# Orders of their own for the last batches of a scan, expert and feed-forward kernel

## The reference

```
delta = softplus(x @ Wd + bd);  B = x @ WB + bB;  C = x @ WC + bC      # 16 states s
h_s   = clip(exp(min(delta * A_s, 2)) * h_s + clip(delta * B_s, -2, 2) * x, -100, 100)
y     = sum_s h_s * C_s + x * D                                       # scan over 1024 tokens
e     = argmax softmax(y @ Wr + br)                                   # 4 experts, the best one
moe   = (silu(y @ up_e + b) @ down_e + b) * weight
x1    = layernorm(x + layernorm(y + moe) * ln_w + ln_b)
out   = layernorm(x1 + (silu(x1 @ wg) * (x1 @ wu)) @ wdn)             # hidden size 384
```

## Time and profile before

| | |
|---|---|
| runs | 948.23, 947.88, 947.88 us; median 947.88 |
| profiled execution | 944.45 us, its span 942.3 us |
| busy in the span | PE 69%, PEld 54%, DVE 73%, ACT 60%, POOL 65% |
| mean granted TensorE clock | 0.825 |
| memory | 157 GB/s over the span |

### The profile page before, as it was taken

The page is one execution under the profiler, slowest core; times in us unless marked ns, Lnnn a source line. Parts: engine busy times, 40 slices in busy tenths (PEclk is TensorE's granted clock), DMA queues, the critical chain, the costliest instruction groups (busy, mean ns, idle before and its releaser), DMA issues.

```text
span 942.3 us, 14125 instructions
## 1 busy us (share of the span) xinstructions
PE 646.6 (69%) x4244; PEld 512.7 (54%) x4296; DVE 687.4 (73%) x1330; ACT 563.5 (60%) x1052; POOL 608.4 (65%) x516
## 2 busy tenths in 40 slices
PE   3345657875889378956896598947894699168244
PEld 1234536763778257844785387725773488157233
DVE  3699998799779987898879977998789784221131
ACT  5553355694867578684859486757864485165223
POOL 0367557578956898488937895689838883650551
PEclk8587767995899779975999589967998599679766
DMA  3333355754556437653665465643755374325200
GB/s 99 120 139 123 133 171 172 262 178 151 191 200 208 157 117 254 191 196 97 209 205 174 154 198 195 203 157 115 254 174 185 107 238 155 107 85 176 62 3 22
DMA packets 82085, 149.30 MB, mean 158 GB/s; under 512 B 9404, under 2 KB 51144, under 8 KB 81992
## 3 DMA queue, kind: packets, MB, share of 16 engines
...
HBM read 132.80 MB, written 15.40 MB: 157 GB/s over the span
## 4 chain that ended last, share of the span: by engine, by line
POOL 26%; DVE 22%; PE 21%; issue 15%; ACT 10%; DMA 3%; another core or an unknown queue 1%; SPq 1%; POOLq 0%; ACTq 0%; DVEq 0%
DVE state L1136 10%; POOL prod L1163 7%; POOL rows_in L1184 4%; PE psU L647 3%; POOL rstd L1206 3%; DVE psB L1127 3%; PE psD L550 3%; ACT hid L798 3%; PE psT L661 3%; DVE moe L1078 2%; PE psU L686 2%; POOL attn L1228 2%; POOL moe L1222 2%; POOL moe L1220 2%; DVE bst L1095 2%
## 5 line engine op out<-in xcount | busy, mean ns | idle before, releaser
L1163 POOL TENSOR_TENSOR prod<-state,c_wide 128x1024 f32<-128x1024 f32 x128 | 308.1, 2416 | 85.1 <-DVE state L1136 66.1
L520 PE MATMUL psB<-parts,sel 128*128 128x512 bf16 x204 | 95.3, 469 | 139.0 <-DVE state L1136 136.9
L1127 DVE TENSOR_TENSOR psB<-dx,psB 128x512 f32<-128x512 f32 x256 | 166.8, 688 | 12.9 <-PE psB L520 2.6
L1136 DVE TENSOR_TENSOR_SCAN state<-decay,state,psB 128x512 f32<-128x512 f32 x128 | 163.9, 1280 | 14.3 <-issue 0.5
L526 PE MATMUL psY<-ident,prod 128*128 128x128 f32 x1024 | 155.5, 305 | 12.1 <-DVE state L1136 6.3
L1136 DVE TENSOR_TENSOR_SCAN state<-decay,psB 128x512 f32<-128x512 f32 x128 | 155.4, 1214 | 0.2
L759 ACT ACTIVATE decay<-delta,a_sb 128x1024 f32<-128x1024 f32 x128 | 141.0, 1143 | 16.9 <-DVE state L1136 11.6
L526 PEld LDWEIGHTS psY<-ident,prod 128*128 128x128 f32 x1024 | 138.3, 160 | 17.1 <-POOL prod L1163 8.8
L798 ACT ACTIVATE hid<-psU,weights 128x128 f32<-128x128 f32 x352 | 99.5, 370 | 49.3 <-PE psU L647 45.5
L520 PEld LDWEIGHTS psB<-parts,sel 128*128 128x128 bf16 x256 | 26.5, 106 | 186.7 <-DVE state L1136 180.5
L661 PE MATMUL psT<-weights,hid 128*128 128x128 f32 x704 | 97.5, 281 | 0.0
...
## 6 DMA issues: line engine op xcount, KB each, us to landing
c_wide<-c_rows SPq DMA_DIRECT2D x128, 512.0 KB
...
```

The source lines that it names most:

```text
L520: pe.matmul(tokens(psB, c, h), sel[:, s, :], parts[:, c.n % 2, h * HALF:h * HALF + c.hw], start=True, stop=True).then_inc(b_ready, 1)
L1127: v.tensor_tensor(tokens(psB, c, h), dx[:, n % 2, h * HALF:h * HALF + c.hw], tokens(psB, c, h), ALU.mult).then_inc(inp_ready, 1)
L1136: v.tensor_tensor_scan(state[:, g % NSTATE, t0:t0 + c.hw], decay[:, g % NDECAY, t0:t0 + c.hw], tokens(psB, c, h), before, ALU.mult, ALU.ad ...
L1163: g_.tensor_tensor(prod[:, g % NPROD, w], state[:, g % NSTATE, w], c_wide[:, g % NC, w], ALU.mult).then_inc(prod_ready, 1)
```

## The change

Each of the five lists at the end gets content: the tasks of the last batch's scans and all that follows. On TensorE, ScalarE, VectorE and GpSimd the resulting sequence first differs from the one before in the last batch (`6 up 0` where `7 add 6` was, `7 decay 11` where `5 x_high 0` was, `5 stats 1 1` where `7 scan 10` was, `5 gather 1` where `7 prod 1` was). SyncE's list at the end begins with `5 c 6`, and its first difference is `6 over` and `4 weights 10` where `5 c 15` and `4 weights 8` were, while batch 5 is scanned. The numbers count from the end: -1 is batch 7, -4 batch 4. Cut to what the prediction speaks of:

```
 PE_LAST = [
...
+    (-3, "ff_up", 1, 2), (-1, "spread", 14, 1), (-3, "ff_up", 1, 3), (-3, "ff_up", 1, 4), (-3, "ff_up", 1, 5),
+    (-3, "ff_down", 1), (-2, "up", 8), (-3, "ff_part", 1, 0), (-2, "down", 7), (-3, "ff_part", 1, 1),
+    (-3, "ff_part", 1, 2), (-1, "spread", 15, 0), (-2, "up", 9), (-2, "down", 8), (-1, "spread", 15, 1),
+    (-1, "add", 12), (-2, "up", 10), (-2, "down", 9), (-2, "down", 10), (-1, "add", 13), (-1, "add", 14),
...
+    (-1, "up", 8), (-2, "ff_part", 1, 1), (-1, "up", 9), (-1, "down", 8), (-1, "up", 10), (-1, "down", 9),
+    (-2, "ff_part", 1, 2), (-1, "down", 10), (-1, "x_turn", 0), (-1, "x_rest", 0), (-1, "ff_up", 0, 0),
...
 ]
 ACT_LAST = [
...
+    (-2, "result", 1), (-2, "sort_copy", 2), (-1, "decay", 13), (-1, "decay", 14), (-1, "decay", 15),
+    (-2, "result", 2), (-3, "norm", 1, 1), (-2, "silu", 3), (-2, "result", 3), (-2, "silu", 4), (-3, "norm", 0, 2),
...
+    (-1, "sort_copy", 0), (-1, "silu", 0), (-1, "result", 0), (-1, "sort_copy", 1), (-1, "silu", 1), (-1, "silu", 2),
+    (-1, "result", 1), (-1, "sort_copy", 2), (-1, "router_exp"), (-1, "result", 2), (-1, "silu", 3),
...
 ]
 DVE_LAST = [
...
+    (-3, "stats", 0, 2), (-1, "scan", 12), (-1, "scan", 13), (-3, "ff_mul", 1, 0), (-3, "ff_mul", 1, 1),
+    (-1, "scan", 14), (-3, "ff_mul", 1, 2), (-3, "stats", 1, 2), (-1, "scan", 15), (-1, "router_shift"),
+    (-1, "slots"), (-2, "combine", 0), (-2, "stats", 0, 0), (-2, "stats", 0, 1), (-2, "combine", 1),
...
 ]
 POOL_LAST = [
...
+    (-3, "rstd", 1, 0), (-1, "prod", 6), (-3, "affine", 1), (-1, "prod", 7), (-1, "prod", 8), (-1, "prod", 9),
...
+    (-3, "rstd", 1, 2), (-1, "prod", 14), (-1, "prod", 15), (-2, "gather", 0), (-2, "gather", 1), (-2, "gather", 2),
+    (-2, "gather", 3), (-2, "gather", 4), (-1, "scatter", 0), (-2, "gather", 5), (-2, "rstd", 0, 0),
+    (-2, "gather", 6), (-2, "gather", 7), (-2, "affine", 0), (-1, "scatter", 1), (-1, "scatter", 2),
...
 ]
 SP_LAST = [
+    (-3, "c", 6), (-3, "c", 7), (-3, "c", 8), (-4, "rows"), (-3, "c", 9), (-3, "c", 10), (-4, "weights", 3),
+    (-3, "c", 11), (-4, "weights", 4), (-4, "x"), (-3, "c", 12), (-4, "weights", 5), (-3, "c", 13),
+    (-4, "weights", 6), (-3, "c", 14), (-4, "weights", 7), (-2, "over"), (-4, "weights", 10), (-3, "c", 15),
+    (-4, "weights", 8), (-4, "weights", 9), (-2, "c", 0), (-4, "store", 0), (-4, "store", 1), (-1, "xT"),
+    (-4, "store", 2), (-2, "c", 1), (-2, "c", 2), (-2, "c", 3), (-2, "c", 4), (-2, "c", 5), (-3, "weights", 0),
+    (-3, "weights", 1), (-3, "weights", 2), (-2, "c", 6), (-2, "c", 7), (-3, "rows"), (-2, "c", 8), (-2, "c", 9),
...
 ]
```

More of the change, by code:

```diff
@@ L144 @@
 PE_LAST = [
+    (-2, "yT_turn"), (-1, "spread", 2, 0), (-1, "spread", 2, 1), (-1, "skip"), (-2, "logits"), (-1, "spread", 3, 0),
+    (-1, "add", 0), (-1, "spread", 3, 1), (-1, "add", 1), (-2, "rank"), (-1, "spread", 4, 0), (-1, "add", 2),
+    (-1, "spread", 4, 1), (-1, "spread", 5, 0), (-1, "spread", 5, 1), (-1, "add", 3), (-1, "spread", 6, 0),
+    (-1, "spread", 6, 1), (-1, "add", 4), (-1, "spread", 7, 0), (-1, "spread", 7, 1), (-1, "spread", 8, 0),
+    (-3, "x_turn", 0), (-1, "spread", 8, 1), (-3, "x_rest", 0), (-3, "ff_up", 0, 0), (-3, "ff_up", 0, 1),
@@ new lines @@
+    (-3, "ff_up", 0, 2), (-3, "ff_up", 0, 3), (-1, "spread", 9, 0), (-3, "ff_up", 0, 4), (-1, "add", 5),
+    (-1, "spread", 9, 1), (-3, "ff_up", 0, 5), (-2, "sort_turn", 0), (-2, "up", 0), (-1, "add", 6), (-2, "up", 1),
+    (-2, "sort_turn", 1), (-1, "spread", 10, 0), (-1, "spread", 10, 1), (-2, "down", 0), (-2, "up", 2),
+    (-2, "down", 1), (-2, "sort_turn", 2), (-1, "spread", 11, 0), (-1, "add", 7), (-1, "spread", 11, 1),
+    (-2, "down", 2), (-1, "add", 8), (-2, "up", 3), (-3, "ff_down", 0), (-1, "add", 9), (-3, "ff_part", 0, 0),
@@ new lines @@
+    (-1, "spread", 12, 0), (-3, "ff_part", 0, 1), (-3, "ff_part", 0, 2), (-2, "up", 4), (-2, "down", 3),
+    (-1, "spread", 12, 1), (-1, "add", 10), (-1, "add", 11), (-2, "down", 4), (-2, "up", 5), (-1, "spread", 13, 0),
+    (-1, "spread", 13, 1), (-3, "x_turn", 1), (-2, "up", 6), (-3, "x_rest", 1), (-2, "down", 5),
+    (-1, "spread", 14, 0), (-3, "ff_up", 1, 0), (-3, "ff_up", 1, 1), (-2, "down", 6), (-2, "up", 7),
+    (-3, "ff_up", 1, 2), (-1, "spread", 14, 1), (-3, "ff_up", 1, 3), (-3, "ff_up", 1, 4), (-3, "ff_up", 1, 5),
@@ new lines @@
+    (-2, "ff_up", 0, 5), (-1, "sort_turn", 0), (-1, "up", 0), (-1, "up", 1), (-1, "sort_turn", 1), (-1, "down", 0),
+    (-1, "up", 2), (-1, "down", 1), (-1, "sort_turn", 2), (-1, "down", 2), (-1, "up", 3), (-2, "ff_down", 0),
+    (-2, "ff_part", 0, 0), (-2, "ff_part", 0, 1), (-2, "ff_part", 0, 2), (-1, "up", 4), (-1, "down", 3),
+    (-1, "up", 5), (-1, "down", 4), (-2, "x_turn", 1), (-1, "up", 6), (-2, "x_rest", 1), (-1, "down", 5),
+    (-2, "ff_up", 1, 0), (-2, "ff_up", 1, 1), (-1, "down", 6), (-1, "up", 7), (-2, "ff_up", 1, 2), (-2, "ff_down", 1),
@@ new lines @@
+    (-2, "ff_up", 1, 3), (-1, "down", 7), (-2, "ff_up", 1, 4), (-2, "ff_part", 1, 0), (-2, "ff_up", 1, 5),
+    (-1, "up", 8), (-2, "ff_part", 1, 1), (-1, "up", 9), (-1, "down", 8), (-1, "up", 10), (-1, "down", 9),
+    (-2, "ff_part", 1, 2), (-1, "down", 10), (-1, "x_turn", 0), (-1, "x_rest", 0), (-1, "ff_up", 0, 0),
+    (-1, "ff_up", 0, 1), (-1, "ff_up", 0, 2), (-1, "ff_up", 0, 3), (-1, "ff_down", 0), (-1, "ff_up", 0, 4),
+    (-1, "ff_up", 0, 5), (-1, "ff_part", 0, 0), (-1, "ff_part", 0, 1), (-1, "ff_part", 0, 2), (-1, "x_turn", 1),
@@ L145 @@
+    (-1, "x_rest", 1), (-1, "ff_up", 1, 0), (-1, "ff_up", 1, 1), (-1, "ff_up", 1, 2), (-1, "ff_up", 1, 3),
+    (-1, "ff_up", 1, 4), (-1, "ff_down", 1), (-1, "ff_up", 1, 5), (-1, "ff_part", 1, 0), (-1, "ff_part", 1, 1),
+    (-1, "ff_part", 1, 2),
 ]
 ACT_LAST = [
+    (-3, "silu", 7), (-4, "gate", 1, 2), (-3, "result", 7), (-3, "silu", 8), (-3, "silu", 9), (-3, "result", 8),
+    (-3, "silu", 10), (-3, "result", 9), (-1, "decay", 0), (-3, "result", 10), (-1, "decay", 1), (-4, "norm", 1, 2),
+    (-2, "y_copy"), (-1, "decay", 2), (-1, "decay", 3), (-2, "yT_copy"), (-1, "decay", 4), (-1, "decay", 5),
@@ new lines @@
+    (-1, "decay", 6), (-1, "decay", 7), (-1, "decay", 8), (-1, "decay", 9), (-3, "norm", 0, 0), (-1, "decay", 10),
+    (-3, "norm", 0, 1), (-1, "decay", 11), (-3, "x_high", 0), (-3, "x_low", 0), (-3, "gate", 0, 0),
+    (-3, "gate", 0, 1), (-3, "gate", 0, 2), (-3, "norm", 1, 0), (-2, "router_exp"), (-2, "sort_copy", 0),
+    (-1, "decay", 12), (-2, "silu", 0), (-2, "silu", 1), (-2, "result", 0), (-2, "sort_copy", 1), (-2, "silu", 2),
+    (-2, "result", 1), (-2, "sort_copy", 2), (-1, "decay", 13), (-1, "decay", 14), (-1, "decay", 15),
@@ new lines @@
+    (-2, "result", 2), (-3, "norm", 1, 1), (-2, "silu", 3), (-2, "result", 3), (-2, "silu", 4), (-3, "norm", 0, 2),
+    (-2, "result", 4), (-2, "silu", 5), (-3, "x_high", 1), (-2, "silu", 6), (-3, "x_low", 1), (-2, "result", 5),
+    (-3, "gate", 1, 0), (-3, "gate", 1, 1), (-2, "silu", 7), (-2, "result", 6), (-3, "gate", 1, 2), (-2, "result", 7),
+    (-2, "silu", 8), (-2, "silu", 9), (-2, "result", 8), (-2, "silu", 10), (-2, "result", 9), (-2, "result", 10),
+    (-3, "norm", 1, 2), (-1, "y_copy"), (-1, "yT_copy"), (-2, "norm", 0, 0), (-2, "norm", 0, 1), (-2, "x_high", 0),
@@ new lines @@
+    (-1, "silu", 7), (-2, "gate", 1, 2), (-1, "result", 6), (-1, "result", 7), (-1, "silu", 8), (-1, "silu", 9),
+    (-1, "result", 8), (-1, "silu", 10), (-1, "result", 9), (-1, "result", 10), (-2, "norm", 1, 2),
+    (-1, "norm", 0, 0), (-1, "norm", 0, 1), (-1, "x_high", 0), (-1, "x_low", 0), (-1, "gate", 0, 0),
+    (-1, "gate", 0, 1), (-1, "gate", 0, 2), (-1, "norm", 1, 0), (-1, "norm", 1, 1), (-1, "norm", 0, 2),
+    (-1, "x_high", 1), (-1, "x_low", 1), (-1, "gate", 1, 0), (-1, "gate", 1, 1), (-1, "gate", 1, 2),
@@ L147 @@
+    (-1, "norm", 1, 2),
 ]
 DVE_LAST = [
+    (-3, "combine", 1), (-3, "stats", 1, 0), (-3, "ff_mul", 0, 0), (-3, "ff_mul", 0, 1), (-3, "ff_mul", 0, 2),
+    (-1, "scan", 9), (-3, "stats", 1, 1), (-1, "scan", 10), (-2, "router_pick"), (-1, "scan", 11),
+    (-3, "stats", 0, 2), (-1, "scan", 12), (-1, "scan", 13), (-3, "ff_mul", 1, 0), (-3, "ff_mul", 1, 1),
+    (-1, "scan", 14), (-3, "ff_mul", 1, 2), (-3, "stats", 1, 2), (-1, "scan", 15), (-1, "router_shift"),
+    (-1, "slots"), (-2, "combine", 0), (-2, "stats", 0, 0), (-2, "stats", 0, 1), (-2, "combine", 1),
@@ new lines @@
+    (-2, "stats", 1, 0), (-2, "ff_mul", 0, 0), (-2, "ff_mul", 0, 1), (-2, "ff_mul", 0, 2), (-1, "router_pick"),
+    (-2, "stats", 1, 1), (-2, "stats", 0, 2), (-2, "ff_mul", 1, 0), (-2, "ff_mul", 1, 1), (-2, "ff_mul", 1, 2),
+    (-2, "stats", 1, 2), (-1, "combine", 0), (-1, "stats", 0, 0), (-1, "stats", 0, 1), (-1, "combine", 1),
+    (-1, "stats", 1, 0), (-1, "ff_mul", 0, 0), (-1, "ff_mul", 0, 1), (-1, "ff_mul", 0, 2), (-1, "stats", 1, 1),
+    (-1, "stats", 0, 2), (-1, "ff_mul", 1, 0), (-1, "ff_mul", 1, 1), (-1, "ff_mul", 1, 2), (-1, "stats", 1, 2),
@@ L149 @@
 ]
 POOL_LAST = [
```

(10 more changed lines are left out.)

12 lines of the change are left out of this document (added), and 6 rows, old and new, of the table SP_LAST.

## The result

The changed kernel takes 966.8 us (median of 4 runs, 964.91 to 968.79); the kernel before, beside it on the same chip, took 948.06 us (4 runs, 947.88 to 949.59). The ratio is 1.0194 [1.0166, 1.0223]: 18.7 us slower. The forecast was 963.7. The profiled execution has a span of 966.2 us, 23.9 over that of before, at a mean granted clock of 0.814.

A forecast was written before the change was run, and what follows sets the result against it. VectorE was taken to bound each batch's scans, and older batches' MoE blocks and FFN its end, through TensorE, ScalarE and weight loads. Terms 8.1 + 3.7 + 1.5 + 1.0 + 1.5 = 15.8 gave 963.7 us, range 953 to 973.

The forecast's parts named there:

- Step 1: Batch 5's last scans: SyncE issues `weights 8` later, so TensorE waits at `up 8`; +8.1 us, bounds +5.7 and +9.5.
- Step 2: After the pause at `up 8`, TensorE's dense work up to scan 15's spread runs at low clock; +3.7 us, bounds 0 and +8.
- B: Same wait at `up 8`, but the clock isn't lost on the path: 960.0 us, chance 0.25.
- C: Clock falls and stays low, so matmuls of 595 to 616 us cost some 8 more: 971.7 us, chance 0.13.
- rival D: Wait for `weights 8` is taken up later in VectorE's gaps ending batches 6 and 7: 951.9 us, chance 0.10.
- E: The clock's low stretches move, giving back 16.6 us against 12.1 lost: 943.4 us, chance 0.05.
- Step 3: Batch 6: SyncE issues `c 8` behind `rows`, so GpSimd's `prod 8` waits; +1.5 us, bounds 0 and +3.
- Step 4: Last batch's scans, all engines: scan 14 delays `ff_mul 1 2`, the other moves cancel; +1.0 us, bounds -2 and +3.
- Step 5: Behind the last batch's scans: GpSimd's scatter run ends later, `router_exp` delays `silu 3`; +1.5 us, bounds -1 and +4.

The follow-up runs named there:

- e1_w10: Kernel before with only SyncE's `over` of batch 6 and `weights 10` of batch 4 ahead of `c 15`, `weights 8` and `weights 9`: 957.24 us, ratio 1.0087.
- e3_sp_only: Kernel before with SyncE's whole new list and the old order on the four other engines: 963.38 us, ratio 1.0137.
- e2_c8: Kernel before with only SyncE's `c 8` of batch 6 moved behind `rows` of batch 5: 953.45 us, ratio 1.0031.
- e6_pool: Kernel before with only GpSimd's new order for the last batch's scans: 954.43 us, ratio 1.0066.
- e5_tail: Kernel before with the new lists of all five engines only behind the last batch's scans: 948.8 us, ratio 1.0018.

## Why the prediction was right, and where not

*Step 1, the wait for `weights 8`.* Right, to the tenth: `up 8` starts 8.1 us later than its 586.52 plus the 2.4 us of drift. Issue was forecast at 588.9 and is 591.34 less 2.4, the same. The load was there 5.7 us after issue, as the burst's third was. The Trainium skill's rule (DMA: Bandwidth & Descriptors, "Queues, rings and completion order"), by which the load might have been done with the first at 3.3, is not contradicted, but this load took the long time here, in e1_w10 and e3_sp_only as well (waits of 7.84 and 7.49).

*Step 2, the clock.* The mechanism was right, the size off: 3.7 forecast. In the trace `up 8` takes 1.0 and the three `ff_part` 1.0 more, and the spread of scan 15 is 10.9 late, 2.8 more than the wait explains; scan 15 itself ends 2.3 beyond it. In finer windows the clock was low from 592.5 to 602.7; it had fallen 4.5 us before work resumed at 597.02, so only 5.7 us of it held work. I had put the whole low stretch behind the pause, as at `x_turn`.

*Both together:* 11.8 forecast; 10.4 at scan 15 and 9.8 at scan 4 of batch 6, as 0.6 us is taken up in gaps; e1_w10 alone 8.3 by the runs and 9.7 by its trace. Rivals B and C had the clock wrong (0.51 for 10 us, then 1.00), rival D's gaps give back no more than this, and nothing of E's time given back shows: the last line of the table keeps all of the lag.

*Step 3, `c 8` behind `rows`.* The mis-sized term: 1.5, bounds 0 and 3, against 3.8 in the trace of after and 3.5 in e2_c8 (2.9 by its runs). My bounds took a c load to land in 3.3 to 5.7 us, from the weight loads. With three row loads ahead and the next c load right behind, the product starts 7.48 (after), 7.16 (e2_c8) and 7.59 us (e3_sp_only) after issue, later than a weight load's 3.3 to 5.7. A load of one row spread to 128 partitions had no landing in the trace of before, and its price was taken from loads of another kind; the bound should have been open upwards.

*Step 4, the last batch's scans.* The step that failed: 1.0 forecast, up to 3, against 5.2 in the trace. "The other moves cancel" was wrong twice. I had cost GpSimd's changed order by queue time only and not by what VectorE does at that moment: the held `chosen` is 2.7 us. And `affine 1` before `prod 7` was to make scan 10 later by 1.9, "hidden by PE". It isn't hidden: from scan 9 to scan 10 the lag grows from 18.6 to 21.5, by 2.9 as in e6_pool. What the forecast did argue from, scan 14 ahead of `ff_mul 1 2`, makes `ff_mul 1 2` (+23.9) and `rstd 1 2` late, but from scan 13 to add 15 the lag falls from 23.2 to 21.9, so no net loss of this move shows. By the runs the four lists cost 4.7 in all, so the term is nearer 3 there (4.7 less e5_tail's 1.7). One reason may be that the hold doesn't come in every execution; with one profiled execution of each kernel that isn't shown.

*Step 5, behind the scans.* 1.5 forecast, 2.0 in the trace, 1.7 by e5_tail. The two table loads take 1.28 us each, and 1.29 pass from the first one's start to the exponential.

The sum was 15.8, against 18.7 in the runs and 21.5 in the trace, where it is made up so: 15.8, less 1.4 for the clock and 0.6 taken up behind scan 15, plus 2.3 for `c 8` and 0.7 more up to scan 15 of batch 6, plus 4.2 for the scans and 0.5 for the tail. The first two steps, three quarters of the forecast, carry it. That SyncE's part comes out so close, 13.3 forecast and 13.0 in e3_sp_only, is partly luck: the clock and the gaps took 2.0 less, and `c 8` 2.3 more.
